# First attention layer of a sandwich kernel: value results in two banks of PSUM, and the steps in which small pieces borrow the second bank

## The reference

```python
Q = (x @ Wq.T).reshape(b, n, H, R)       # H = 8 heads, R = 64
K = (x @ Wk.T).reshape(b, n, H, R)
V = (x @ Wv.T).reshape(b, n, H, d)       # d = 128
attn = jnp.einsum('bnhr,bmhr->bhnm', Q, K)
attn = jax.nn.softmax(attn, axis=-1)
out = jnp.einsum('bhnm,bmhd->bnd', attn, V)   # summed over the heads
```

## Time and profile before

| | |
|---|---|
| median of 3 runs | 1346.72 us (1346.33 to 1348.34) |
| profiled execution: its own time | 1347.51 us |
| profiled execution: span | 1345.7 us |
| mean granted TensorE clock | 0.963 |
| PE busy | 1217.2 us (90%) |
| PE weight load busy | 687.3 us (51%) |
| DVE busy | 992.6 us (74%) |
| ACT busy | 815.4 us (61%) |
| POOL busy | 378.6 us (28%) |
| share of PE in the chain that ended last | 71% |

### The profile page before, as it was taken

How to read it: one execution, slowest core, us unless ns; L and a number is a source line. 1 busy time by engine, 2 the same in 40 slices (tenths; PEclk the granted TensorE clock), 3 DMA queues, 4 the chain that set the end, 5 groups by cost and what they waited for, 6 DMA issues and landing times.

```text
span 1345.7 us, 22173 instructions
## 1 busy us (share of the span) xinstructions
PE 1217.2 (90%) x7985; PEld 687.3 (51%) x7985; DVE 992.6 (74%) x2073; ACT 815.4 (61%) x1617; POOL 378.6 (28%) x304
## 2 busy tenths in 40 slices
PE   6899999989999889998789999998889989799987
PEld 4366666656666643333233333333456754477653
DVE  5778978879778357767767767776689867888855
ACT  5866866757667224342256666666668863588851
POOL 0000000001000023344420000003488851698823
PEclk9799999999999999998589999999999999899999
DMA  6567667757676700003123321100011110011101
GB/s 158 125 152 161 157 147 173 161 122 180 138 164 158 166 1 0 14 32 103 26 82 106 83 44 44 44 3 23 23 25 33 33 25 0 13 35 36 29 16 32
DMA packets 54104, 103.29 MB, mean 77 GB/s; under 512 B 14994, under 2 KB 29532, under 8 KB 52572
## 3 DMA queue, kind: packets, MB, share of 16 engines
q1 hardware_dynamic: 53996, 101.88, 32.1%
HBM read 21.16 MB, written 5.44 MB: 20 GB/s over the span
## 4 chain that ended last, share of the span: by engine, by line
PE 71%; DVE 14%; ACT 4%; issue 4%; POOL 2%; SPq 2%; DMA 1%; POOLq 0%; DVEq 0%; ACTq 0%
PE ps L712 14%; PE ps L732 7%; PE ps L1046 5%; PE ps L1005 5%; PE ps L1026 4%; PE ps L1103 4%; SPq L552 2%; PE ps L878 2%; PE ps L698 2%; PE ps L1155 2%; PE ps L872 2%; PE ps L1209 2%; PE ps L1177 2%; PE ps L1238 2%; PE ps L862 2%
## 5 line engine op out<-in xcount | busy, mean ns | idle before, releaser
L2263 ACT ACTIVATE probsT<-ps 128x512 f32<-128x512 f32 (+1 forms) x304 | 163.8, 577 | 99.7 <-PE ps L1030 88.3
L1448 DVE TENSOR_REDUCE negmax<-ps 128x1 f32<-128x1024 f32 x128 | 153.5, 1204 | 51.1 <-PE ps L732 51.1
L2449 POOL TENSOR_SCALAR rstd<-mv 128x4 f32<-128x4 f32 (+1 forms) x31 | 7.1, 230 | 522.9 <-DVE mv L1382 522.7
L732 PE MATMUL ps<-k_st,q_st 64*128 64x512 f32 x512 | 132.9, 639 | 11.1 <-ACT d_sq L2097 5.5
L2097 ACT ACTIVATE d_sq<-ps,negmax 128x1024 f32<-128x1024 f32 x86 | 95.8, 1114 | 72.8 <-DVE negmax L1448 70.1
L1005 PE MATMUL ps<-arena 84*128 84x512 bf16 (+3 forms) x384 | 113.7, 357 | 25.4 <-DVE cmax L1710 23.3
L712 PE MATMUL ps<-probsT,v_nat 128*128 128x256 f32 x512 | 120.1, 388 | 11.5 <-DVE yT L1442 8.6
L1710 DVE CUSTOM_DVE_ANT_0 q_st<-ps,rel 128x256 f32<-128x256 f32 (+7 forms) x128 | 96.7, 756 | 44.5 <-PE ps L1005 43.5
L712 PE MATMUL ps<-probsT,v_st 128*128 128x256 f32 x512 | 120.0, 387 | 5.9 <-DVE yT L1439 3.2
L1710 DVE CUSTOM_DVE_ANT_0 k_st<-ps,rel 128x256 f32<-128x256 f32 (+7 forms) x128 | 96.8, 756 | 37.2 <-PE ps L1005 36.7
L712 PEld LDWEIGHTS ps<-probsT,v_nat 128*128 128x128 f32 x512 | 96.4, 192 | 45.4 <-issue 30.1
(11 more groups left out here) (236 smaller groups left out, 2587.0 us busy)
## 6 DMA issues: line engine op xcount, KB each, us to landing
probsT<-arena SPq DMA_DIRECT2D x336, 128.0 KB, 2.4
probsT<-probs SPq DMA_DIRECT2D x176, 128.0 KB, 2.4
probsT<-probsT SPq DMA_DIRECT2D x62, 128.0 KB, 2.4
arena<-c_q_parts SPq DMA_DIRECT2D x8, 576.0 KB
arena<-c_k_parts SPq DMA_DIRECT2D x8, 576.0 KB
arena<-in_L_ffn_w_dram SPq DMA_DIRECT2D x3, 512.0 KB
arena<-in_c_far_dram SPq DMA_DIRECT2D x16, 96.0 KB
work<-in_L_ffn_wqkv_dram SPq DMA_DIRECT2D x1, 1536.0 KB, 10.9
```

The costliest lines, as they stand in the source:

```text
L732: ins = pe.matmul(ps[:, pair(m, 4 + 2 * i + head) + n, :], q_st[r:r + R0, i * P:(i + 1) * P], k_st[r:r + R0, n * CH:(n + 1) * CH], start=T ...
L1448: dve.tensor_reduce(negmax[:, u:u + 1], s2, AX_X, ALU.max, negate=True).then_inc(s_a_negmax, 1)
L2263: act.activation(c_p[:, kt % 2, j0:j0 + heads, q0 - kt * P:q0 - kt * P + n], ps[:, 4 + c % 2, 0:heads * n].rearrange("p (h n) -> p h n", n ...
```

## The change

Chunk n goes to bank 6 + n % 2. Its wait is for `s_a_oadd >= n - 1` from n = 2 on, which says that chunk n-2 is out. Odd chunks now share bank 7 with the strewn pieces. So the pieces move to slots in which an odd chunk has just been taken out, each behind a wait for that (`s_a_oadd >= 2, 8, 16, 18, 22, 24`). The odd chunk after a piece waits until the piece has been read out: chunk 3 for the bias, 9 and 23 for ACT's copies of transposes, 17 and 19 for DVE's layernorm of the result, and 25 for the gate's shift.

The bias product moves from slot 13 to 11, the input transposes from 20 and 22 to 22 and 23, the result transposes from 39 and 41 to 38 and 42 (their layernorm on DVE from 40 and 42 to 39 and 43), the next input transposes from 49 and 50 to 50 and 51, and the gate from 53 to 54 (its shift on DVE from 54 to 55). In the stretch after slot 63 the two `turn_g` go from beside chunk 29 to behind `shared_up(1)`, into banks 4 and 5, and PE's wait for both of ACT's copies of them stands ahead of `shared_down(0)`.

```diff
--- before.py
+++ after.py
@@ -706,10 +706,25 @@
                 if k0 == 0:
                     if head == 0:
                         pe.wait_ge((s_a_evA, s_a_evB)[c % 2], TURNED * (2 * m + c // 2 + 1))
-                        if 4 * m + c >= 1:
-                            pe.wait_ge(s_a_oadd, 4 * m + c)
+                        n = 4 * m + c
+                        if n >= 2:
+                            pe.wait_ge(s_a_oadd, n - 1)
+                        else:
+                            pe.wait_ge(s_ft, 9)
+                        if n == 3:
+                            pe.wait_ge(s_c_by, 1)
+                        if n == 9:
+                            pe.wait_ge(s_xT, group_no(0, 1, 1))
+                        if n == 17:
+                            pe.wait_ge(s_yn, group_no(0, 0, 0))
+                        if n == 19:
+                            pe.wait_ge(s_yn, group_no(0, 0, 1))
+                        if n == 23:
+                            pe.wait_ge(s_xT, group_no(1, 0, 1))
+                        if n == 25:
+                            pe.wait_ge(s_gshift, 1)
                 for kt in range(k0, k1):
-                    ins = pe.matmul(ps[:, 6, 0:HC],
+                    ins = pe.matmul(ps[:, 6 + c % 2, 0:HC],
                                     a_v[m % 2][:, kt, head * P:(head + 1) * P],
                                     a_pT[:, c % 2, :, head, kt, :], start=(head == 0 and kt == 0),
                                     stop=(head == 1 and kt == QT - 1), skip_group_check=True)
@@ -760,28 +775,32 @@
                     turn_f(2 * slot + 1)
                 if slot == 4:
                     turn_f(8)
-                if slot == 13:
+                if slot == 11:
+                    pe.wait_ge(s_a_oadd, 2)
                     pe.wait_ge(s_ld_c, 16 * 10)
                     pe.wait_ge(s_ft, 9)
                     pe.matmul(ps[:, 7, 0:1], nat3[:, 3, :], b3n[:, 2:3], start=True, stop=True).then_inc(s_c_bp, 1)
-                if slot == 20:
-                    pe.wait_ge(s_c_by, 1)
+                if slot == 22:
+                    pe.wait_ge(s_a_oadd, 8)
                     half_in(0, 1, 0, 7)
-                if slot == 22:
+                if slot == 23:
                     pe.wait_ge(s_xT, group_no(0, 1, 0))
                     half_in(0, 1, 1, 7)
-                if slot == 39:
+                if slot == 38:
                     pe.wait_ge(s_a_oadd, 16)
                     half_out(0, 0, 0, 7)
-                if slot == 41:
+                if slot == 42:
+                    pe.wait_ge(s_a_oadd, 18)
                     pe.wait_ge(s_yn, group_no(0, 0, 0))
                     half_out(0, 0, 1, 7)
-                if slot == 49:
+                if slot == 50:
+                    pe.wait_ge(s_a_oadd, 22)
                     half_in(1, 0, 0, 7)
-                if slot == 50:
+                if slot == 51:
                     pe.wait_ge(s_xT, group_no(1, 0, 0))
                     half_in(1, 0, 1, 7)
-                if slot == 53:
+                if slot == 54:
+                    pe.wait_ge(s_a_oadd, 24)
                     gate(0, 0)
                     gate(0, 4)
 
@@ -908,17 +927,17 @@
 
             k = QT * BLOCKS - LATE
             weigh_half(k, 0, 8)
-            turn_g(0, 0, 7)
             weigh_half(k + 1, 0, 8)
-            pe.wait_ge(s_gT, 1)
-            turn_g(0, 1, 7)
             weigh_half(k + 2, 0, 8)
             weigh_half(k + 3, 0, 8)
             pe.wait_ge(s_a_exp, NU * BLOCKS)
             shared_up(0)
             shared_up(1)
+            turn_g(0, 0, 4)
+            turn_g(0, 1, 5)
             weigh_half(k + 4, 0, 8)
             weigh_half(k + 5, 0, 8)
+            pe.wait_ge(s_gT, 2)
             shared_down(0)
             pe.wait_ge(s_a_oadd, 4 * BLOCKS)
             half_out(0, 1, 0, 5)
@@ -1434,7 +1453,7 @@
                 b, p = n // (4 * PAIRS), n // 4 % PAIRS
                 dve.wait_ge(s_a_pv, n + 1)
                 y = yT[:, b * SEQ + (n % 4) * HC:b * SEQ + (n % 4 + 1) * HC].rearrange("p (t g q) -> p g t q", t=2, g=4)
-                o = ps[:, 6, 0:HC].rearrange("p (g t q) -> p g t q", g=4, t=2)
+                o = ps[:, 6 + n % 2, 0:HC].rearrange("p (g t q) -> p g t q", g=4, t=2)
                 if p == 0:
                     dve.tensor_copy(y, o).then_inc(s_a_oadd, 1)
                 else:
@@ -1527,17 +1546,17 @@
                 if slot == 23:
                     dve.tensor_copy(sel[:, :, :, :], sel_f[:, :, :, :]).then_inc(s_selc, 1)
                 for g in range(HALF):
-                    if slot == 39 + 2 * g:
+                    if slot == 38 + 4 * g:
                         out_stats(0, 0, g, 7)
                         half_aggr(0, g)
-                    if slot == 40 + 2 * g:
+                    if slot == 39 + 4 * g:
                         half_norm(0, 0, g, 7, spread_no("out", 0, 0, g))
                     if slot == 44 + g:
                         in_stats(1, 0, g)
                         half_aggr(0, g)
                     if slot == 47 + g:
                         half_xn(1, 0, g, spread_no("in", 1, 0, g))
-                if slot == 54:
+                if slot == 55:
                     gate_shift(0)
                 if slot == 56:
                     gate_scores(0)
@@ -2138,8 +2157,8 @@
                 if m + 1 < BLOCKS:
                     a_evac_v(m + 1)
                 divide(m, NU - 1)
-            turned_g(0, 0, 7)
-            turned_g(0, 1, 7)
+            turned_g(0, 0, 4)
+            turned_g(0, 1, 5)
 
             def shared(k):
```

## The result

The first timing gave a median of 1333.4 us (1329.05 to 1334.51, 4 runs) against 1346.53, a ratio of 0.9894 with a 95% interval of 0.987 to 0.9918. A second timing gave 1334.24 (1331.43 to 1335.5, 5 runs) against 1346.48, ratio 0.9907, interval 0.9893 to 0.992. With one more run, the ten executions have a median of 1333.9: 12.6 us faster. The forecast was 1336.0, a gain of 10.8. So the direction and most steps held, and the gain was forecast too small, by 1.8 us against the ten executions and by 2.3 against the first timing. That first timing lies at the lower edge of the stated range of 1333 to 1342: its median is just inside, and its ratio, 0.9894 of 1346.53, is 1332.3 and just outside.

What follows compares the result with a forecast made beforehand. PE, 90% busy, was taken to bound the kernel. 12.8 us removed less 1.7, 0.8 and 0.5 left 9.8; plus 1.0 after slot 63, 10.8 off 1347.51: 1336.7, stated as 1336.0 for the median, range 1333 to 1342.

Steps and rivals of the forecast that it cites:

- The waits that go: Up to slot 63: with two banks PE's waits for add_out vanish, 10.2 us, and scores after boundaries don't wait.
- So 10.2 us go: Term for add_out waits up to slot 63: 15.5 us in all, less 5.13 + 0.17 after it.
- the two rivals on DMA landings: Chunk DMAs: landings replace the bank's waits, 1346.7 us, chance 0.06; or landings slow to 14 us, 1350, chance 0.06.
- The 2.61 at slot 39: Boundary of slot 39: moving the result transposes removes the 2.61 us by which the next scores came late.
- The new waits: New PE waits: 1.7 us before slot 24's scores, 0.7 at chunk 19, 0.1 on later scores, 0.5 at chunk 23.
- After slot 63: Chunks 29 to 31: 1.0 us gained, 32.5 against 33.5 from slot 63's end to chunk 31's end.
- the low clock on chunk 30: After a 4.3 us idle wait for DMAs, the clock drops in chunk 30, charged 1.6 us.
- The rival of half the gain: Boundaries and later slots: DVE nearly full, so scores wait for exponentials; gain 5.5 us, 1341.2, chance 0.17.

Runs made afterwards that it cites:

- e_xn: Kernel before, with DVE's second half of the input normalisation moved from slot 19 to slot 20; one execution, 1346.45 us.
- e_onebank: Changed kernel, pieces at their new slots, but every chunk in bank 6, waiting for the add_out of the chunk before; ratio 0.9986.
- e_best: Changed kernel, slot 23's ACT copy behind values, stretch after slot 63 filled, slot 43's layernorm and slot 51's copy put earlier; 1329.32 us, ratio 0.9877.
- e_fill: Changed kernel, with both shared_up and the gate transposes between chunks 29 and 30; ratio 0.989.
- e_both: Changed kernel, slot 23's ACT copy behind the new values, both shared_up and the gate transposes between chunks 29 and 30; 1331.62 us, ratio 0.9877.
- e_both2: Second run of changed kernel with slot 23's ACT copy behind values, shared_up and gate transposes between chunks 29 and 30; 1331.19 us, ratio 0.989.
- e_act: Changed kernel, with ACT's copy of slot 23's input transposes behind its copy of the new values; 1335.22 us, ratio 0.9911.

## What of the prediction held, and the step that failed

*The waits that go.* Right in kind, short in size. The slot behind a boundary went from 6.56 to 5.57 us, the three waits of slots 58 to 62 are gone, and the scores after a boundary did not wait. The step that failed is the count, "So 10.2 us go": this term of the sum was too small, and it measured 11.6. The count took over from the view who ended each wait, and the view had put the 0.99 before chunk 7 down to a DMA. But `add_out`, behind a piece of 1.07 us, held PE there for nearly as long: moving the piece took 0.8 of the 0.99 away (`e_xn`), and in the changed kernel the whole wait is gone. With it 11.2 us of waits go, and 0.4 more because each of these slots was some hundredths longer than its wait says. The balance then closes: 11.6 + 2.6, less 1.68, 0.64, 0.47 and 0.17 for the new waits and 0.66 for late landings, is 10.6, as the first profile has it. The 0.99 was also what spoke for the two rivals on DMA landings, and only some 0.2 of it was a landing's.

*The 2.61 at slot 39* was right, and `e_onebank` isolates it. *The new waits* were right in place and size: 1.68 for 1.7, 0.64 and 0.17 for 0.7 and 0.1, and 0.47 for 0.5. Late landings cost another 0.2 to 0.7 (0.17 and 0.49 in the first profile), for which I had charged nothing. Slots 8 to 63 gained 10.6, 10.9 and 11.1 in three profiles, and the forecast was 9.8: too low by 0.8 to 1.3.

*After slot 63* the forecast was 1.0, and it was 1.5, 3.2 and 1.5. The mechanism was right: chunk 29 at once, chunk 30 at 12.0 behind the end of slot 63, a low clock, chunk 31 free. Three sizes were off. Chunk 29 waited 1.3 to 1.9 for its DMAs and not 0.4, which costs nothing, since chunk 30 waits for its own anyway. What stands behind chunk 30 was rated 0.5 too long: `shared_up` and `turn_g` took 4.15 us and not 4.4, and chunk 31 took 7.07 and not 7.3. This is the 0.5 by which two profiles beat the forecast. And I had put the low clock on chunk 30 in every execution; in one of three it fell on chunk 29 and was free.

*The rest.* The layer's gain is thus 12.1, 14.1 and 12.6 by profile, which agrees with the 12.6 of the ten executions. The first profile's additional 3 us before slot 8 and its loss of 2.1 after chunk 31 are scatter: slot 0 comes before every edit and began anywhere from 18.1 to 19.6 us in the profiles. The first timing's 13.1 us, against 12.6 over the ten executions, holds some scatter too. *The rival of half the gain* was tested by the boundaries and fell. What it named, DVE's lag, cost 0.17 us in slot 47 of the changed kernel and 0.4 + 0.3 in `e_best`.

What stays open: why the part after chunk 31 takes from 865.8 to 871.2 us with the same instructions. In the profiles it went with how long the low clock lasted there, summed from the granted clock: 73.8 and 77.3 us in the two profiles with 865.8, 84.1 to 84.2 in the five with 868.3 to 868.5, and 90.7 to 90.8 in the three with 870.6 to 871.2. But no run varied that alone.

## What to carry to other kernels

A second PSUM bank paid here because the reader of the first stood behind other work in its own queue: look at what the evacuating engine has in front of the evacuation, not at the evacuation's 0.4 us. A piece placed at a block's boundary is best put behind the evacuations in each engine's queue: moving one copy in ACT's order took 1.75 us off the boundary, of which 0.27 came back in the next slot. When two events end within some tenths of each other, the named releaser is one of two (here `add_out` and a landing, 0.16 us apart): check the other before counting a wait out.

## What the runs showed of the hardware

The granted clock fell to its lower level of 1.2 GHz after waits of quite different lengths: in the changed kernel on chunk 30 after 3.43 us of idle time in one execution, on chunk 29 after 1.89 us in another, while the same kernel's waits of 1.34 and 1.84 us before chunk 29 and 1.19 before chunk 30 left it at 2.4 GHz. Before chunk 31 it fell after 2.14 us in `e_fill` and not after 1.94, 2.02 and 1.80 us in `e_both`, `e_both2` and `e_best`. So the length of the one wait did not decide it in these profiles. 32 matmuls of a chunk took 8.86 us with such a stretch in them and 7.17 without. Where it falls decides the price: 1.7 us on chunk 30, and nothing on chunk 29, whose delay is spent waiting anyway.

The ten executions of the changed kernel span 1329.05 to 1335.8 us, 0.5%. The 1.75 us that `e_act` took off one boundary were plain in the slots of one profile and could not be seen in the median of its five executions.
